# Issuing the steady state's loads and stores from SyncE instead of GpSimd

## The reference

```python
x = x + _L0_cond_ref(x, cond_1024, ...)     # mixture of experts
x = x + _L1_cond_ref(x, cond_1024, ...)     # gate
x = x + _L2_cond_ref(x, cond_1024, ...)     # adapted MLP
def step(H, xs):                            # L3, 512 of them in a row
    Z = sigmoid(xz + H @ Whz.T + bhz)
    R = sigmoid(xr + H @ Whr.T + bhr)
    H_tilda = tanh(xh + R * H @ Whh.T + bhh)
    H_new = Z * H + (1.0 - Z) * H_tilda
    Y = H_new @ Whq.T + bhq
```

## Time and profile before

| | |
|---|---|
| median of three runs | 1318.87 us (1318.06 to 1318.91) |
| the profiled execution | 1317.63 us |
| span of its trace | 1315.6 us |
| PE busy | 1273.4 us (97%) |
| DVE busy | 883.3 us (67%) |
| ACT busy | 444.5 us (34%) |
| POOL busy | 119.8 us (9%) |
| mean granted clock of PE | 0.969 |

### The profile page before, as it was taken

One profiled execution on the slowest core, in us unless ns is written; L12 is line 12 of the kernel. 1 busy time (PEld: TensorE's weight loads), 2 busy tenths in 40 slices (PEclk: granted clock), 3 DMA queues, 4 the chain that ended last, 5 costly groups with the idle time before them and its releaser, 6 DMA issues.

```text
span 1315.6 us, 54396 instructions
## 1 busy us (share of the span) xinstructions
PE 1273.4 (97%) x22767; PEld 1224.5 (93%) x22768; DVE 883.3 (67%) x5664; ACT 444.5 (34%) x2246; POOL 119.8 (9%) x120
## 2 busy tenths in 40 slices
PE   6989999999999999999999999999999999999975
PEld 6389999999999999999999999999999999999864
DVE  3436777667777776777777667777776777677655
ACT  1013333333333333333333333333333333333322
POOL 2410000000000000000000000000000000000000
PEclk9999999999999999999999999999999999999855
DMA  9400000000000000000000000000000000000000
GB/s 350 147 7 3 10 11 11 11 11 8 6 10 11 11 10 11 11 7 7 10 11 11 11 11 7 6 11 11 11 10 11 11 7 7 10 11 7 6 6 6
DMA packets 8822, 27.87 MB, mean 21 GB/s; under 512 B 2920, under 2 KB 3376, under 8 KB 7296
## 3 DMA queue, kind: packets, MB, share of 16 engines
q1 hardware_dynamic: 5280, 15.41, 3.2%
q0 software_dynamic: 3296, 8.98, 2.3%
HBM read 19.94 MB, written 4.19 MB: 18 GB/s over the span
## 4 chain that ended last, share of the span: by engine, by line
PE 91%; DVE 4%; ACT 1%; DMA 1%; issue 1%; SPq 1%; POOL 0%; DVEq 0%; POOLq 0%
PE bank L367 52%; PE gate_rh L367 29%; PE gate_z L367 10%; ACT rg L701 1%; DMA own<-in_own 1%; DVE rhp L936 1%; DVE x L857 1%; DVE state L952 0%; ACT hin L701 0%; SPq L280 0%; DVE zsum L941 0%; DVE rhp L943 0%; DVE rh L937 0%; DVE osb L876 0%; DMA low<-wrow 0%
## 5 line engine op out<-in xcount | busy, mean ns | idle before, releaser
L701 ACT ACTIVATE rg<-gate_rh 128x16 f32<-128x16 f32 x512 | 93.7, 183 | 513.9 <-PE gate_rh L367 513.9
L367 PEld LDWEIGHTS gate_rh<-state,whp 128*128 128x128 f16 x6144 | 231.8, 97 | 23.9 <-DVE state L952 15.9
L367 PEld LDWEIGHTS gate_rh<-rhp,whp 128*128 128x128 f16 x6144 | 230.2, 96 | 18.0 <-DVE rhp L936 10.0
L367 PE MATMUL gate_rh<-state,whp 128*128 128x8 f16 x6144 | 233.1, 167 | 14.0 <-DVE state L952 13.8
L367 PE MATMUL gate_rh<-rhp,whp 128*128 128x8 f16 x6144 | 239.1, 167 | 7.1 <-DVE rhp L936 7.1
L936 DVE SCALAR_TENSOR_TENSOR rhp<-rg,hist 128x16 f16<-128x16 f32 x512 | 89.0, 174 | 214.8 <-ACT rg L701 203.2
L367 PE MATMUL gate_z<-state,whp 128*128 128x16 f16 x4096 | 180.4, 177 | 0.0
L701 ACT ACTIVATE zg<-zsum 128x16 f32<-128x16 f32 x512 | 110.6, 216 | 169.8 <-DVE zsum L941 169.8
L367 PE MATMUL bank<-xt,rw 128*128 128x128 f32 x1024 | 159.9, 290 | 5.4 <-DVE sa L837 4.4
L946 DVE TENSOR_SCALAR zin<-zg,nsscale 128x16 f32<-128x16 f32 x512 | 125.8, 246 | 56.4 <-ACT zg L701 47.2
L367 PE MATMUL bank<-xt,sw 128*128 128x128 f32 x1024 | 153.1, 289 | 0.0
(11 more groups left out here) (153 smaller groups left out, 1815.0 us busy)
## 6 DMA issues: line engine op xcount, KB each, us to landing
aw<-in_aw SPq DMA_DIRECT2D x4, 2048.0 KB, 19.5
xt<-in_xT POOLq DMA_DIRECT2D x32, 128.0 KB, 2.6
out<-osb POOLq DMA_DIRECT2D x32, 128.0 KB, 2.2
rw<-in_rw SPq DMA_DIRECT2D x2, 1024.0 KB, 11.6
sw<-in_sw SPq DMA_DIRECT2D x3, 512.0 KB, 7.9
wh<-in_wh SPq DMA_DIRECT2D x3, 256.0 KB, 10.0
wx<-in_wx SPq DMA_DIRECT2D x3, 256.0 KB, 18.3
l1w<-in_l1w POOLq DMA_DIRECT2D x2, 256.0 KB, 4.4
```

The costliest lines, as they stand in the source:

```text
L367: return pe.matmul(o, w, x, start=start, stop=stop, skip_group_check=True)
L701: return act.activation(o, i, f, **kw)
```

## The change

Every load of `xt` and every store of `osb` is issued by SP. The loads of block 0 and block 1 stand between the weights in SP's order, the first one after `aw1`, the second after `rw2` and before `iota`. The load of block 2 stands ahead of the four groups of `low<-wrow`, behind a wait for `x1_done`; before, POOL issued it after scaling `wx`. SP gets a body with the waits and the order of the loads and stores of POOL's, and the final wait. POOL keeps `exp_scores`.

```diff
             sp.dma_start(aw1[:], a["aw1"]).then_inc(ad_in, 16)
+            sp.dma_start(xt[:, 0], a["xT"][:, :, 0:TOK]).then_inc(x_in[0], 16)
             sp.dma_start(sw1[:], a["sw1"]).then_inc(l0w_in, 16)
...
             sp.dma_start(rw2[:], a["rw2"]).then_inc(l0r_in, 16)
+            sp.dma_start(xt[:, 1], a["xT"][:, :, TOK:2 * TOK]).then_inc(x_in[1], 16)
             sp.dma_start(iota[:], a["iota"]).then_inc(const_in, 16)
...
+            def load_x(m, par):
+                at = token_start(m)
+                sp.dma_start(xt[:, par], a["xT"][:, :, at:at + TOK]).then_inc(x_in[par], 16)
+
+            def store(m):
+                at = token_start(m)
+                sp.wait_ge(out_done, count(m, 1))
+                sp.dma_start(out[:, :, at:at + TOK], osb[:]).then_inc(stored, 16)
+
+            sp.wait_ge(x1_done, 1)
+            load_x((0, 2), 0)
             for at, i in enumerate(LOW_ORDER):
                 sp.wait_ge(wrow_dve, 4 * (at + 1))
...
+            def body(m, par, has_y, has_l23, has_l0):
+                if m[1] + 3 < BLOCKS:
+                    sp.wait_ge(x1_done, count(later(m, 1), 1))
+                    load_x(later(m, 3), 1 - par)
+                if has_y:
+                    store(later(m, -1))
+
+            blocks(body)
+            store((0, BLOCKS - 1))
+            sp.wait_ge(stored, 16 * BLOCKS)
...
-            pool.dma_start(xt[:, 0], a["xT"][:, :, 0:TOK]).then_inc(x_in[0], 16)
-            pool.dma_start(xt[:, 1], a["xT"][:, :, TOK:2 * TOK]).then_inc(x_in[1], 16)
...
-            pool.wait_ge(x1_done, 1)
-            load_x(2 * TOK, 0)
             exp_scores((0, 1))
 
             def body(m, par, has_y, has_l23, has_l0):
-                if has_l0 and not (type(m[0]) is int and m[1] + 3 >= BLOCKS):
-
-                    x_block = xcols(later(m, 3))
-                    pool.wait_ge(x1_done, count(later(m, 1), 1))
-                    load_x(x_block, 1 - par)
                 if has_l0:
                     exp_scores(later(m, 2))
-                if has_y:
-                    store(later(m, -1))
 
             blocks(body)
-            store((0, BLOCKS - 1))
-            pool.wait_ge(stored, 16 * BLOCKS)
```

More of the change, by code:

```diff
@@ L322, in _ @@
             pool.tensor_scalar(wqh[:], wq[:], qscale[:], None, ALU.mult).then_inc(split_w, 1)
[L324 to L335, removed]
             pool.wait_ge(wx_in, 16 * 3)
```

## The result

| | before | changed |
|---|---|---|
| median | 1318.87 us (1317.04 to 1319.42) | 1315.58 us (1314.75 to 1316.89) |
| ratio to before, 95% interval | | 0.9979 (0.9971 to 0.9987) |
| profiled execution | 1317.63 us | 1314.75 us |
| span of its trace | 1315.6 us | 1312.6 us |
| POOL busy | 119.8 us | 73.6 us |

The change is faster by 0.21%, 2.8 us by the ratio (1.7 to 3.8). In two later comparisons on other chips the same kernel had 0.9981 (0.9972 to 0.9990) and 0.9977 (0.9968 to 0.9986). The forecast was 1318.6 us, 0.3 us less, with a range that ended at 1316.9: the direction was right and the size was not.

The account below looks back on a forecast made before the run. PE's work and its order were taken to bound the steady state, with setup and the last store at the ends. Steady state 0, constants 0, block 2's load 0 and last store -0.3 gave 1318.6 us, range 1316.9 to 1320.4.

Parts of the forecast that it names:

- The steady state, "Cost: 0": Blocks' steady state: moving 29 loads and 31 stores from POOL's queue to SP's, both off the chain, costs 0.
- Rival 1: Steady state: POOL's descriptors do cost it, 1.67 us in eight longer steps, so 1316.9 us; chance 0.08.
- Setup, "So I take 0": Setup's constants: `own` lands as before, since the bytes ahead of it stay the same; 0, bounds -0.6 and +1.0 us.
- the end that I had put at 256 KB by 406 GB/s: Setup's constants: lower bound, -0.6 us, if the input blocks held up the weights more from a second queue.
- rival 3: Setup: the path through the constants moves by the issues alone, +1.0 us, 1319.6 us; chance 0.15.
- Rival 2: Setup: SP's queue becomes the bound, two loads of 2.44 us each, chain 4.9 us late, 1323.5 us; chance 0.07.
- the cover that I had named: Setup, load of block 2: 7 us between SP's last weight issue and its first copy of `low`; cost 0.
- The last store, -0.3: End of the kernel: SP starts the last store 0.26 us sooner after DVE, no further gain; -0.3 us in all.
- My bound of -0.7: Last store: the most it could gain, 0.7 us, if SP's 1.88 us to the landing holds whatever the size.
- rival 5: Last store: SP's whole path to the landing is the shorter one, the -0.7 us bound, 1318.2 us; chance 0.12.
- The sum: Whole kernel: 0 + 0 + 0 - 0.3 = -0.3 us, by the median 1318.6 us.
- rival 4: Block 30, clock at 1.2 GHz: one step earlier or later is 0.9 us either way, 1317.7 to 1319.5; chance 0.10.

Follow-up runs that it names:

- the placements behind `own`: The changed kernel with the load of block 1 right behind `own`, 0.9976, or behind the last weight (`bq`), 0.9982.
- the two half-and-half kernels: The kernel before with only the body's 31 stores on SP, 1.0003, or only the 29 loads of blocks 3 to 31 on SP, 1.0017.

## Why the prediction was wrong

**The steady state, "Cost: 0", right; its reason, wrong.** I wrote that line 857 was "the first that such a cost would hit" and let its steady 0.417 us stand for all. The body's loads start beside it and do not stretch it. I did not look at what else ran beside POOL's issues. Beside the stores that is `zin`, line 946, 0.45 us instead of 0.23 in 29 of the 32 bodies. The page had it in plain sight, a mean of 246 ns before and 233 after for 512 executions. The Trainium skill (SBUF — State Buffer, "Who interferes with whom") counts `tensor_scalar` with the instructions that can enter a two-port mode and then lock GpSimd out or wait for it, and `zin` is one, with a single SBUF tensor as input; the trace agrees in that POOL's store stretches it and SP's does not. Which mode `zin` ran in, no run here shows. Rival 1's price was 1.67 us for the stretched steps. Seven of the eight are still there in the changed kernel and last as long. The eighth, the last step of block 27, up to the first state of block 28, was POOL's: the load of block 31 starts 0.30 us ahead of `zin` and stretches it to 0.41, and the step takes 2.94 us. So it does in the four traces in which the load falls there, and 2.83 in the 14 others:

```profile
1157.90 0.73 POOL L330 DMA_DIRECT2D xt<-in_xT  x1 [32.52 <-DVE x L851]
1158.20 0.41 DVE L946 TENSOR_SCALAR zin<-zg,nsscale 128x16 f32<-128x16 f32 x1
```

That is 0.11 us of the 1.67, once. What the stores cost is 0.14 us in step 1, of which step 2 gives back 0.13, since PE has a slack there: 0.01 us a block, 0.3 us over the kernel. Over 17 traces, the seven with the body's whole stores on POOL have 1024.89 to 1025.42 us for blocks 1 to 27, median 1025.2, and the ten with them on SP 1024.44 to 1025.31, median 1024.6; the sum of the small rests is 0.6 us. One of the ten (the load of block 1 behind the last weight) is as long as the others' longest, and the two kernels that moved only one kind of the body's DMAs are 0.1 apart, so 0.6 is a tendency and no constant, and no run gives a cause to more than 0.4 of it.

**Setup, "So I take 0".** Over the traces, the score starts at 18.80 to 20.18 us in the eight with the first loads on POOL, 19.25 in the mean, and at 18.30 to 19.32 in the seven with both on SP ahead of `iota`, 18.65 in the mean. That is -0.6, the end that I had put at 256 KB by 406 GB/s. The two sets overlap and the placements behind `own` gave 18.30 and 19.71, so the cause isn't shown; what is shown is that the landing differs by about 1 us between executions, and that +1.0 for the later issue, rival 3, did not come: `own` was issued up to 1.4 us later. Rival 2, slower by 4.9 us, did not come either: SP needed 0.70 and 0.66 us for the two loads and not 2.44. The load of block 2 was issued in 0.55 us at 38.71, well inside the cover that I had named. (That cover was counted a little high: the eighth copy of `low` started at 51.68 us and not at 51.5, so 1.15 of the 1.7 us would have been covered and not 1.3.)

**The last store, -0.3, mis-sized: -1.0.** This is the step that failed by experiment. The start was right (0.26 forecast, 0.25 measured), and the landing nearly so, 2.1 us on SP and 2.2 on POOL. What failed is that I ended the sum at the landing. The earlier trace rows have the landing at 1314.5 and the span ends at 1315.6: 1.1 us behind it, of which the changed kernel has 0.4. The difference is the DRAIN of the engine that waits last, 0.65 us on POOL and 0.01 on SP (line 57, above). My bound of -0.7 was drawn from SP's shorter landing and did not hold this either. Moving the wait alone gave 0.5 us of tail, moving the store with it 0.9. The rule of the Trainium skill (DMA: Bandwidth & Descriptors, "Latency and other measured facts") on the first byte, which I had as rival 5, is not what did it: the packets of SP's last store begin 1.2 us after the start of the issue, and POOL's 1.3, where the rule has 0.4 us between them. In a slice view of 0.09 us of the changed kernel, from 1309 us on, they start in slice 25, at 1311.25:

```profile
GB/s 0 0 0 0 0 0 0 0 0 0 0 0 0 0 0 0 0 0 0 0 0 0 0 0 0 142 313 296 284 273 143 6 0 0 0 0 0 0 0 0
```

**The sum.** Tail 1.0, landing of the constants 0.6 and blocks 0.6 are 2.2 us, where the ratio has 2.8 and, in the last comparison, 3.0, each give or take 1.1. Two of the three terms I had at zero, and each one's other end was in the text; the range took them as if they could not all fall on one side. Only the tail is shown by experiment; the other two are differences between sets of traces that overlap. What remains, 0.6 to 0.8 us, is within the intervals, and no trace assigns it.

**The clock,** rival 4: block 30 took 39.08 to 40.98 us in the traces, whatever the kernel, and the low stretch of setup about 3, 7 or 10 us. With the latter goes the piece from the score to the first state: 76.5 to 76.9 us in the six traces with 3 us, 76.6 to 77.2 in the three with 7, 77.4 to 78.0 in the eight with 10. So single traces differ by 1 us or two for no reason of this change; the 3.0 us between the two first spans have 0.6 of it.

**Left open.** Why POOL's DRAIN at the end takes 3.1 to 3.3 us in the two half-and-half kernels and the one with quartered stores, 0.65 in both traces of the kernel before and with the first two loads on SP, and 0.48 with the last store alone put back on POOL. The number of DMAs that POOL issued doesn't order them: 37, 39 and 164 in the long ones, 66 and 68 at 0.65 us, 5 at 0.48. And whether the first loads, or chance, brought `own` forward.

## What to carry to other kernels

A kernel's time ends at the last instruction, not at the last landing: read the piece behind the last DMA as well, by the DRAIN of each engine too, and ask which engine waits last. When a DMA moves from GpSimd's queue to another, look at every instruction of VectorE that runs beside it, by its longest and not by its median duration, and then whether the stretch reaches the engine that is the bound. And when several terms of a sum are set to zero with a bound each, let the range hold them on one side; here the better find lay beside the change, in the order of the weights: three small constants ahead of 3.5 MB of weights were worth some 7 us, the higher clock behind them included.

## What the runs showed of the hardware

- A store of 128 partitions issued by GpSimd stretches a one-input `TENSOR_SCALAR` of VectorE from 0.23 to 0.45 us; one of 32 partitions to 0.28 to 0.30 us; a load to 0.41 us where it starts 0.30 us ahead of it, to 0.29 at 0.43 us, and not at all at 0.49.
- From the end of VectorE's last instruction to the end of the program it takes 2.5 to 2.9 us with the store and the wait on SyncE (ten traces), 3.5 to 3.8 with both on GpSimd (four), 3.0 with the store on GpSimd and the wait on SyncE, and 6.0 to 7.4 in three kernels more. Between the landing of the last store and the end stands the DRAIN of the engine that waits last: 0.01 us on SyncE, 0.48, 0.65 or 3.1 to 3.3 us on GpSimd; why GpSimd's differs is open.
- In the kernel before, TensorE's clock fell to 1.2 GHz at 26.6 us, after it had been idle from 21.5 to 25.5 us, for 6.8 us; in the other traces with such a gap of 3.3 to 4.0 us it fell in the gap or at most 1.1 us behind it, for 3 to 10 us. With the constants first, where no gap up to 60 us was longer than 1.1 us, it stayed at 2.4 GHz.
- The same 32 KB transfer behind the same weights landed anywhere from 18.2 to 20.1 us.
